# A linear recurrence carried by groups of four tokens, with one output table

## The reference, cut

```python
x = x + 0.5 * ffn(layernorm(x), gate_w, w1, w2)
x = x + attn(layernorm(x), a_params, B_w, C_w, D)
x = x + 0.5 * ffn(layernorm(x), gate_w, w1, w2)

def attn(u, a_params, B_w, C_w, D):            # the recurrence
    lambdas = cayley_circulant_eigenvalues(a_params, 128)   # all of modulus 1
    Bu = einsum('bsd,nd->bsn', u, B_w)
    def step(h, bu_t):
        Wh = ifft(lambdas * fft(h)).real
        return (Wh + bu_t,) * 2
    _, hs = scan(step, zeros((8, 128)), swapaxes(Bu, 0, 1))
    return einsum('sbn,dn->bsd', hs, C_w) + D * u

def ffn(inputs, gate_w, w1, w2):               # E = 8 experts, F = 512, CAP = 160
    tokens = inputs.reshape(-1, 128)           # only the first 160 tokens of an expert are served
    probs = softmax(tokens @ gate_w); expert_idx = argmax(probs)
    mask1 = one_hot(expert_idx, E); pos = cumsum(mask1, axis=0) - 1
    ...                                        # per expert: relu(t @ w1) @ w2, scaled by probs
```

## Time and profile before

| | us |
|---|---|
| median of 3 runs (range) | 189.78 (189.37 to 195.57) |
| the profiled execution, first to last instruction (its only time) | 192.7 |
| TensorE busy | 157.3 (82%) |
| VectorE busy | 103.8 (54%) |
| ScalarE busy | 61.1 (32%) |
| GpSimd busy | 87.6 (45%) |
| DMA, mean rate | 84 GB/s |

### The profile page before, as it was taken

How to read it: one execution, slowest core, us unless ns; L and a number is a source line. 1 busy time by engine, 2 the same in 40 slices (tenths; PEclk the granted TensorE clock), 3 DMA queues, 4 the chain that set the end, 5 groups by cost and what they waited for, 6 DMA issues and landing times. The chain is left out here.

```text
span 192.7 us, 2709 instructions
## 1 busy us (share of the span) xinstructions
PE 157.3 (82%) x882; PEld 111.4 (58%) x882; DVE 103.8 (54%) x341; ACT 61.1 (32%) x144; POOL 87.6 (45%) x90
## 2 busy tenths in 40 slices
PE   6999689989999772994977977778689896999930
PEld 3124456469998431351844864656589544999920
DVE  1043954624385202739369679999992813345330
ACT  3311241334636000474156445343110003463300
POOL 2400001774006760427677797597330037722782
PEclk9999996999999997599699999999955999999995
DMA  5999900121900115900021101011010101210110
GB/s 136 352 371 329 280 6 2 41 54 41 435 3 29 57 53 171 269 0 0 0 56 54 58 0 54 10 48 54 0 56 0 54 17 41 54 27 14 45 54 27
DMA packets 17309, 16.16 MB, mean 84 GB/s; under 512 B 1520, under 2 KB 14448, under 8 KB 17264
## 3 DMA queue, kind: packets, MB, share of 16 engines
q1 hardware_dynamic: 15648, 13.11, 22.4%
q0 software_dynamic: 1280, 2.62, 4.6%
q10 hardware_dynamic: 368, 0.26, 0.7%
HBM read 12.59 MB, written 5.51 MB: 94 GB/s over the span
## 5 line engine op out<-in xcount | busy, mean ns | idle before, releaser
L760 PE MATMUL bank<-warm_in,ones_bf 128*128 128x512 bf16 x121 | 34.0, 424 | 6.7 <-DMA x<-x_scratch 4.5
L760 PEld LDWEIGHTS bank<-warm_in,ones_bf 128*128 128x128 bf16 x121 | 12.1, 108 | 25.8 <-issue 10.5
L293 POOL DMA_INDIRECT xg<-x,tok x10 | 10.2, 1021 | 27.4 <-DVE tok L602 24.7
L340 POOL TENSOR_TENSOR zs<-z,st 128x512 f32<-128x512 f32 x8 | 14.2, 1770 | 16.5 <-DVE z L732 16.5
L890 PE MATMUL bank<-hT,w2s 128*128 128x160 f32 x128 | 20.2, 301 | 0.9 <-ACT hT L398 0.9
L879 PE MATMUL bank<-xcT,w1s 128*128 128x160 f32 x128 | 20.7, 305 | 0.0
L948 PE MATMUL bank<-g,zc 128*128 128x128 f32 x56 | 12.1, 300 | 8.6 <-issue 5.8
L890 PEld LDWEIGHTS bank<-hT,w2s 128*128 128x128 f32 x128 | 17.8, 190 | 1.4 <-issue 0.7
L398 ACT ACTIVATE hT<-bank 128x320 f32<-128x320 f32 x32 | 13.7, 435 | 15.3 <-PE bank L879 13.8
L879 PEld LDWEIGHTS bank<-xcT,w1s 128*128 128x128 f32 x128 | 18.0, 190 | 0.8 <-ACT xcT L390 0.8
L293 POOL DMA_INDIRECT xg<-out,tok x10 | 10.1, 1006 | 16.1 <-DVE tok L602 13.3
(11 more groups left out here) (154 smaller groups left out, 295.3 us busy)
## 6 DMA issues: line engine op xcount, KB each, us to landing
xt<-x_turned SPq DMA_DIRECT2D x8, 256.0 KB, 5.6
w1s<-w SPq DMA_DIRECT2D x2, 1024.0 KB, 8.6
w2s<-w SPq DMA_DIRECT2D x8, 256.0 KB, 7.3
x<-x_scratch SPq DMA_DIRECT2D x8, 256.0 KB, 4.6
out<-x SPq DMA_DIRECT2D x8, 256.0 KB, 2.3
cl<-const_late SPq DMA_DIRECT2D x1, 256.0 KB, 5.9
ce<-const_early ACTq DMA_DIRECT2D x1, 254.0 KB, 4.7
xg<-x,tok POOLq DMA_INDIRECT x10, 2.5
```

The lines of the kernel that those rows point to most:

```text
L293: pool.indirect_dma_start(xg[:, j, :], None, (x_rows, out_rows)[n], bass.IndirectOffsetOnAxis(ap=tok[:, j:j + 1], axis=0), bounds_check=T ...
L340: nc.gpsimd.tensor_tensor(zs[:, b % 2, :], z[:, :], st[:, 0:SEQ], ALU.mult).then_inc(zs_r, 1)
L760: M(bank[to][:, :], ones_bf[:, :], warm_in[:, :], start=True, stop=True)
```

## The change

The tokens of a batch are laid out with token 4p + c in partition p ("(p c)"): a group of four tokens is one partition. The recurrence then runs over NG = 128 groups instead of 512 tokens:

- TensorE sums the four tokens of a group, each through its own table `vt[:, k]` (`group_sums`, four matmuls of 128 columns into one bank), so that the scan, its turns and the states are 128 columns long. `ct` and `st` now count groups; `c1` and `s1` hold one to four steps.
- The value with swapped halves is no longer a second product. ScalarE copies each half of the bank into the other half of `vq` (`turned_part`), and VectorE writes the halves of `zs` crosswise (`carry`). GpSimd turns `vb` and `zc`, VectorE adds `state` = `zc` + `zs`.
- The scan's output is shifted by one group (`z[:, 0]` is zero), so `state` is the one from before the group. What happens inside a group goes straight from the inputs by one table `tab` (`within_groups`, six matmuls of 144 to 280 columns): the products of one, two and three steps, D times u, and the gate. The outward table `gt` has four parts for the four tokens (`read_out`, two matmuls of 272 columns). Both sum in a pair of banks, two pairs in turns.
- GpSimd's `ud` and `w` go. The gate's logits for the second pass come from the same sums (8 further columns for each token; the part that depends on x1 is the gate of u, scaled back by the deviation, `gate_back`), so `turn_x2`, `copy_xT` and `gate_x2` go.
- Setup: other tables (`lagged_inputs`, `outward_tables`), the `keep_warm` calls between the gate's matmuls go, four of the eight `center_w1` steps stand before `place` and four behind it, and 4 warm-up matmuls stand ahead of `slots(0)` instead of 18. `powers` runs two levels ahead of `mark`, five behind `index`, two in `slots(0)`.
- The copy of x to `x1_scratch` no longer waits for the last gather.
- Order within the tokens changes, so `rank` uses other masks, three matmuls instead of two. `PIECES[1]` is cut at batches 3 and 6 instead of 2 and 6.

```diff
-            return rows[b * SEQ:(b + 1) * SEQ, :].rearrange("(c p) d -> p c d", p=P)
+            return rows[b * SEQ:(b + 1) * SEQ, :].rearrange("(p c) d -> p c d", c=TB)
...
-            sp.wait_ge(d_gather[NS - 1], 16)
             sp.dma_start(x1_dram, x_rows).then_inc(d_fill, 16)
             sp.wait_ge(d_fill, 16)
...
-            def turn_back(b):
+            pool.wait_ge(turns, 1)
+            for b in range(NB):
...
-                nc.gpsimd.tensor_tensor(vb[:, :], vq[:, :], st[:, 0:SEQ], ALU.mult).then_inc(vb_r, 1)
-
-            def turn_forth(b):
+                nc.gpsimd.tensor_tensor(vb[:, :], vq[:, :], st[:, 0:NG], ALU.mult).then_inc(vb_r, 1)
...
-
-            for i in range(-1, NB):
-                if i >= 0:
-                    turn_back(i)
-                if i + 1 < NB:
-                    skip_product(i + 1)
-                if i >= 0:
-                    turn_forth(i)
-                if i + 1 < NB:
-                    skip_sum(i + 1)
+                if b >= 1:
+                    pool.wait_ge(state_r, b)
+                nc.gpsimd.tensor_tensor(zc[:, :], z[:, 0:NG], ct[:, 0:NG], ALU.mult).then_inc(zc_r, 1)
...
+            for e in range(E // 2):
+                copy_w1(e)
+            act.wait_ge(vt_ps, 1)
+            nc.scalar.copy(vt[:, :, :], bank[5][:, :].rearrange("p (j f) -> p j f", j=TB)).then_inc(vt_sb, 1)
+            act.wait_ge(k_ps, 1)
+            nc.scalar.copy(tab[:, E + PITCH:E + 2 * PITCH], bank[4][:, PITCH:2 * PITCH])
+            nc.scalar.copy(tab[:, E + 2 * PITCH:E + 4 * PITCH], bank[6][:, 0:2 * PITCH]).then_inc(k_sb, 1)
+            for e in range(E // 2, E):
+                copy_w1(e)
...
+            def turned_part(b):
+
+                act.wait_ge(v_ps, b + 1)
+                if b >= 1:
+                    act.wait_ge(vb_r, b)
+                v = bank[5][:, 0:NG]
+                nc.scalar.copy(vq[0:P // 2, :], v[P // 2:P, :])
+                nc.scalar.copy(vq[P // 2:P, :], v[0:P // 2, :]).then_inc(vq_sb, 1)
...
-            for i in range(-2, NB + 2):
-                if 0 <= i < NB:
...
-                    nc.scalar.copy(vq[:, :], bank[5][:, :]).then_inc(vq_sb, 1)
+            deviation(0)
+            deviation(1)
+            normalise(0)
+            copy_uT(0)
+            normalise(1)
+            for i in range(NB):
+                turned_part(i)
+                if i + 1 < NB:
+                    copy_uT(i + 1)
                 if i + 2 < NB:
                     deviation(i + 2)
-                if 0 <= i + 1 < NB:
...
-                    nc.scalar.copy(uT[:, (i + 1) % 2, :], bank[0][:, :]).then_inc(uT_sb, 1)
-                if i + 2 < NB:
                     normalise(i + 2)
...
-            for k in range(len(PIECES[0])):
...
-                make_hot(0, k)
-            powers(2, 3)
+            mark(0, 0)
+            make_hot(0, 0)
+            lagged_inputs()
             index(0)
-            powers(3, 7)
+            outward_tables()
+            powers(ct, st, 0, 5)
...
+            def turn_back(b):
+
+                dve.wait_ge(vq_sb, b + 1)
+                V.tensor_tensor(va[:, :], bank[5][:, 0:NG], ct[:, 0:NG], ALU.mult).then_inc(va_r, 1)
...
+                V.tensor_tensor_scan(z[:, 1:NG + 1], va[:, :], vb[:, :], 0.0, ALU.add, ALU.add).then_inc(z_r, 1)
+                dve.wait_ge(z_r, b + 1)
+                for h in range(2):
+                    src, dst = slice((1 - h) * P // 2, (2 - h) * P // 2), slice(h * P // 2, (h + 1) * P // 2)
+                    ins = V.tensor_tensor(zs[dst, :], z[src, 0:NG], st[src, 0:NG], ALU.mult)
+                ins.then_inc(zs_r, 1)
+
...
+                V.tensor_tensor(state[:, b % 2, :], zc[:, :], zs[:, :], ALU.add).then_inc(state_r, 1)
...
+                V.tensor_tensor(x2[:, b * TB:(b + 1) * TB, :].rearrange("p (h r) d -> p h r d", h=2), y_of(b)[:, :, :, 0:D],
+                                x1[:, b * TB:(b + 1) * TB, :].rearrange("p (h r) d -> p h r d", h=2),
                                 ALU.add).then_inc(x2_r, 1)
...
+            def gate_back(b):
...
+                for r, at_ in enumerate((0, E + 2 * PITCH)):
+                    ins = V.tensor_tensor(part_of[:, :, r, :], y_pair(b)[:, :, at_:at_ + E],
+                                          sd[:, :, r:r + 1].broadcast_to([P, 2, E]), ALU.mult)
+                link(ins)
+                V.tensor_tensor(lgs[:, b * TB:(b + 1) * TB, :].rearrange("p (h r) e -> p h r e", h=2),
+                                y_of(b)[:, :, :, D:PITCH], part_of, ALU.add).then_inc(y_read, 1)
+
...
+            for i in range(NB):
+                turn_back(i)
                 if i + 2 < NB:
                     stats(i + 2)
-                if 0 <= i < NB:
-                    dve.wait_ge(v_ps, i + 1)
-                    V.tensor_tensor(va[:, :], bank[4][:, :], ct[:, 0:SEQ], ALU.mult).then_inc(va_r, 1)
-                if i == NB - 1:
-                    mark(1, 1)
+                carry(i)
+                turn_forth(i)
                 if i >= 1:
                     add_back(i - 1)
+                    gate_back(i - 1)
                 if i + 2 < NB:
                     shift(i + 2)
-                if 0 <= i < NB:
...
+            mark(1, 1)
+            gate_back(NB - 1)
+            mark(1, 2)
+            add_back(NB - 1)
             make_hot(1, 1)
-            mark_last()
-            finish_last()
             make_hot(1, 2)
...
-                    if b + 1 < TURNED[k][1]:
-                        keep_warm(2)
...
-            center_w1(2, 4)
+            center_w1(0, E // 2)
             place(0, 0)
-            center_w1(4, E)
-            pe.wait_ge(tables, 3)
-            keep_warm(18)
+
...
+            pe.wait_ge(gg_sb, 1)
+            for k in range(TB):
+                ins = nc.tensor.transpose(bank[5][:, k * P:(k + 1) * P], xj[:, k, :], ident)
+            ins.then_inc(vt_ps, 1)
+            for k in range(TB):
...
+                ins = M(bank[4 + 2 * (k // 2)][:, at_:at_ + PITCH], xj[:, k, :], gg[:, 0, :], start=True, stop=True)
+            ins.then_inc(k_ps, 1)
+            center_w1(E // 2, E)
+            pe.wait_ge(vt_sb, 1)
+            pe.wait_ge(k0_sb, 1)
+            keep_warm(4, 2)
             slots(0)
...
+            def group_sums(b):
...
+                for c in range(TB):
+                    ins = M(bank[5][:, 0:NG], vt[:, TB - 1 - c, :],
+                            uT[:, b % 2, c * P:(c + 1) * P], start=(c == 0), stop=(c == TB - 1))
+                ins.then_inc(v_ps, 1)
...
+            def within_groups(b):
...
+                y = y_pair(b)
+                ut = [uT[:, b % 2, c * P:(c + 1) * P] for c in range(TB)]
+                M(y[:, 0, 0:E + 2 * PITCH], ut[0], tab[:, 0:E + 2 * PITCH], start=True, stop=False,
+                  skip_group_check=True)
+                M(y[:, 1, E:E + 2 * PITCH], ut[0], tab[:, E + 2 * PITCH:E + 4 * PITCH], start=True, stop=False,
...
+                  skip_group_check=True)
+                M(y[:, 1, E + PITCH:2 * E + 2 * PITCH], ut[3], tab0[:, :], start=False, stop=False,
+                  skip_group_check=True).then_inc(lag_ps, 1)
+
...
+                y = y_pair(b)
+                for h in range(2):
+                    ins = M(y[:, h, E:E + 2 * PITCH], state[:, b % 2, :],
+                            gt[:, 2 * h:2 * h + 2, :].rearrange("p r c -> p (r c)"), start=False, stop=True,
+                            skip_group_check=True)
                 ins.then_inc(y_ps, 1)
...
             pe.wait_ge(row_sb, NS)
-            keep_warm(27)
+            pe.wait_ge(out_table, 1)
+            keep_warm(24, 6)
             pe.wait_ge(d_x1[0], 16)
-            keep_warm(15)
+            keep_warm(14, 6)
             turn_u(0)
-            keep_warm(2)
...
-                M(bank[4][:, :], bt[:, 0:P], uT[:, i % 2, :], start=True, stop=True)
-                M(bank[5][:, :], bt[:, P:2 * P], uT[:, i % 2, :], start=True, stop=True).then_inc(v_ps, 1)
-                if i == NB - 1:
-                    gate_x2(i - 2)
+                group_sums(i)
+                if i + 1 < NB:
+                    turn_u(i + 1)
                 if i >= 1:
                     read_out(i - 1)
-                if i + 1 < NB:
-                    turn_u(i + 1)
-                if i == 0:
-                    keep_warm(6, 6)
+                within_groups(i)
                 if i == ROUTE_FROM + 2:
                     rank(1, 0)
                 if i == ROUTE_FROM + 4:
...
             rank(1, 1)
-            gate_w()
-            gate_x2(NB - 2)
-            read_out_last()
+            read_out(NB - 1)
             place(1, 1)
             rank(1, 2)
-            keep_warm(8, 6)
+            keep_warm(8, 0)
             place(1, 2)
-            keep_warm(16, 6)
+            keep_warm(16, 0)
             slots(1)
```

(27 more changed lines are left out.)

401 lines of the change are left out of this document (171 added, 230 removed).

## The result

| | before | after |
|---|---|---|
| median of the runs | 190.92 us (189.37 to 195.57, 4 runs) | 177.34 us (176.67 to 178.92, 4 runs) |
| span of the profiled execution | 192.7 us | 175.4 us |
| last `va` | 136.96 | 117.01 |
| token list of the second pass complete | 156.00 | 136.01 |

The ratio is 0.932, 95% interval 0.925 to 0.940: faster, by 13.6 us in the medians, by 17.3 in the two traces. Single executions of one kernel differ by up to 8.6 us, the longer ones mostly at a lower mean granted clock of TensorE, and the ratios compare the faster ones.

The account below looks back on a forecast made before the run. No engine was taken as the limit end to end; chains of waits were. Setup -9.2, before the first `va` -0.4, recurrence -6.3 and tail +0.7 sum to -15.2: 189.78 becomes 174.6 us, 8-in-10 range 168.5 to 181.

Parts of the forecast that it names:

- rival of a half clock throughout: Loop: TensorE at half clock, 9.1 us of matmuls set each round; 194.3 us in all; chance 0.03.
- Recurrence, -6.3: Loop, first to last `va`: VectorE's list plus ScalarE's `u` and `vq`, 7.0 us a round; 45.6 us against 51.9.
- the rule that it quotes: Loop: VectorE instructions with two SBUF inputs and GpSimd instructions reading SBUF block each other whole; 0.95 us for halves and `zc`.
- Before the first `va`, -0.4: Stretch ahead of the loop: one warm-up less, but `u` of batch 1 stands ahead of `vq`; -0.4 us.
- Setup, -9.2: Setup to first scatter: first gathered tile 5.3 us sooner, copy of x 3.9; -9.2 us, bounds -5 and -11.
- The pairs: Setup's gate stage: without the warm-up pairs between and behind gate matmuls, logits complete 3.5 us sooner.
- the copy: First scatter: it can start when its tile is there, 54.9 instead of 58.74 by the old clock; -3.9 us.
- the rival in which setup gives half: Setup: TensorE's clock half behind the gate stage, token list 2 us later; about 179 us in all; chance 0.14.
- Tail, +0.7: Last `va` to second token list: 19.7 us instead of 19.0, with eight warm-ups at half clock; +0.7 us.
- The second experts are not touched: Second experts, behind the tail: not touched by the change, no term in the sum.
- The rival of a clock that falls in the loop: Loop: TensorE's clock falls now and then, rounds of 7.7 us; 179.5 us in all; chance 0.16.
- Routing was hidden behind ScalarE: Loop: routing pieces of at most about 2 us stand behind `snb`, where VectorE waits 2.2 us for ScalarE.

Follow-up runs that it names:

- a5: Kernel after with the product `zc` moved from GpSimd to VectorE, behind the halves of `zs`: 180.33 us, ratio 0.940.
- a2: Kernel after with the next batch's reciprocal and `snb` placed ahead of the residual and logits on VectorE: 171.94 us, ratio 0.897.
- c3: c2 with the next batch's reciprocal and `snb` moved up to between the scan and the halves of `zs`: 166.18 us, ratio 0.864.
- b1: Kernel before with only the copy of x issued early, without its wait for the last gather: 187.06 us, ratio 0.976.
- b2: Kernel before with setup's warm-ups cut: seven pairs around the gate matmuls out, 4 instead of 18 ahead of the first gathered tile: 188.06 us, ratio 0.982.
- a3: Kernel after with the counting of the last piece ahead of the placing of the piece before it, in TensorE's tail: 178.16 us.
- a6: Kernel after with the seven warm-up pairs of the old gate stage put back: 183.08 us, ratio 0.953.
- c2: Kernel after with `snb` ahead of the residual, last counting ahead of placing, more warm-ups in tail, setup and at loop start: 169.41 us.

## Why the prediction was right, and where it was off

The forecast was 174.6, measured 177.3. Of the 2.7 us between them 1.1 is the base, 189.78 from three executions, where four give 190.92. The prediction also took the profiled execution for 2.9 us above that base; it compared a span with a time, and by the estimate above it was 4.7. Its rival of a half clock throughout equals the kernel before from 8.5 us a round on by its own sum (13.7 us over seven rounds), not 8.8.

- **Recurrence, -6.3: the path right, VectorE's list mis-sized.** It was to be 4.8 us and took 4.18; ScalarE's 2.2 took 2.20. A round is 6.46, not 7.0, the loop 42.7, not 45.6, so the term is -9.2. I had added durations of instructions that hand nothing to each other: `va` and statistics, `state` and residual, residual and logits overlap by 0.05 to 0.1 us each. The turns forth took 0.75 to 0.8 instead of 0.95: `zc` begins with the halves, and they slow each other without excluding each other whole. Together they end in 0.75 us, where the halves (0.57 in a5) and a product of 128 columns on GpSimd (`vb`, 0.46) add up to 1.03. What the prediction drew from the rule that it quotes, that the halves and `zc` cannot overlap, is not borne out: the rows of the round show them side by side. a2 and c3 confirm the path.
- **Before the first `va`, -0.4: right size, by luck.** It read -0.7 in the traces, the sum of two parts. `u` of batch 1 ahead of `vq` costs 1.4 against the 7.2 us of b1 and b2, which have the old loop. And 2.2 came back, most likely since TensorE no longer idles 4.49 us for x1 (the copy of x, above); that part the prediction did not have.
- **Setup, -9.2: right sum in this pair of traces, other parts.** -10.0 in the profiled executions, and part of it is luck: that of the kernel before was long here. Its second `center_w1` group took 5.13 us, partly at half clock, and its first gathered tile came at 39.77; in b1, with the same instructions there, it is 3.79 us and 37.97. The pairs were worth 5.7, not 3.5, but `gate_last` costs 1.0 more and the first gate products came later, so that the logits are complete 3.9 sooner; the copy gave 3.2 to 3.6, not 3.9. Other executions with this setup reach x1 at 67.1 to 69.5 instead of 65.7; there the first `center_w1` group takes 4.9 to 6.3 us, partly at half clock, instead of 3.85. So the rival in which setup gives half has part of its way in most profiled executions.
- **Tail, +0.7:** 0.0. The half clock and the eight warm-ups are there as said.
- **"The second experts are not touched", put at nothing, was the step that failed in the profiled execution.** No instruction there is, but the clock was half from 142 to 149 us and cost 2.7. It fell somewhere in that stage in 4 of the 14 profiled executions (a3, a6, c2 and the kernel after, 35.8 to 37.6 us; the others, the kernel before among them, 33.1 to 34.4). All four have the new loop, as eleven of the 14 do. So it may be chance and not the change, and I can't tell which.
- **The rival of a clock that falls in the loop** did not occur: from the second round on, the clock of the kernel after was whole, with 1.63 us of idle in each round. Only its first round was at half clock. Routing was hidden behind ScalarE, as predicted, and showed in c3.

In sum, 13.6 us of the 15.2 forecast came in the medians. The loop gave 2.9 more and the tail cost 0.7 less than I said; setup gave 0.5 to 3 less in most profiled executions, against a base that was itself long by some 2 us, and the clock behind the tail takes some in a few. So the total is nearer than its terms. How much of the last two there is in the medians, four executions don't settle.

## What to carry to other kernels

When an operation becomes four times smaller, look for the ring of in-order lists that now sets the round, and ask of each short instruction in it who waits for it: two instructions moved ahead of a residual were worth 5 us, over a third of what the whole rewrite gave. Take the base of each term from more than one execution, or from a neighbour that has the same stretch. Ask of a wait what stands idle behind it, since the clock that falls there is paid for later. Count the columns that a warm-up keeps from running side by side, not only its own time.

## What the runs showed of the hardware that I had not expected

- Matmuls with 32-column weights for different quarters overlap: three products of 512 fp32 columns took 1.06 us, one alone 1.04; with full-width warm-ups between them, 4.1.
- Weight loads with a stride between columns are slower. The tile `xt`, first in the kernel before, then in the kernel after, whose token order makes the columns four apart:

```profile
L807 PEld LDWEIGHTS bank<-gate_c,xt x8: 190/192/192, 18.0 to 18.7; 128*128 128x128 f32 x8
```

```profile
L842 PEld LDWEIGHTS pair<-gate_c,xt x8: 329/330/331, 13.1 to 14.7; 128*128 128x128 f32 x8
```

  Eight of them hold the logits back by 1.0 us, at full clock too.
- One program, executed four times, got mean clocks from 0.884 to 0.916 and times 7.4 us apart (b2).
